# Splitting a weight-rounding step into a third that stays in place and two thirds that are issued later, in the first stage of an attention and mixture-of-experts kernel

## What is computed

```
xn = layernorm(x)
x  = x + attn0(xn) + ffn0(xn)      # attn0: 16 heads, latent projections, softmax, causal
                                   # ffn0: router, top 4 of 8 experts, gate/up, down
xn = layernorm(x)
x  = x + attn1(xn) + ffn1(xn)      # attn1: sparsemax; ffn1: grouped attention, then top 2 of 8 experts
```

## Time and profile before

| | |
|---|---|
| median of 3 runs | 3134.1 us (3131.94 to 3136.5) |
| the profiled execution | 3129.51 us, span of the core 3127.6 us |
| PE busy over the span | 2809.4 us (90%) |
| DVE, ACT, POOL busy | 2133.4 (68%), 1615.2 (52%), 1506.6 (48%) us |
| granted TensorE clock | 0.956 of full speed over the span, 0.79 in 60 to 350 us |
| in 60 to 350 us | PE busy 228.3 of 290 us, DVE 221.6, POOL 206.7, ACT 138.1 |

### The profile page before, as it was taken

The page is one execution under the profiler, slowest core; times in us unless marked ns, Lnnn a source line. Parts: engine busy times, 40 slices in busy tenths (PEclk is TensorE's granted clock), DMA queues, the critical chain, the costliest instruction groups (busy, mean ns, idle before and its releaser), DMA issues. The chain is left out here.

```text
span 3127.6 us, 61182 instructions
## 1 busy us (share of the span) xinstructions
PE 2809.4 (90%) x20990; PEld 2275.6 (73%) x20990; DVE 2133.4 (68%) x6013; ACT 1615.2 (52%) x3388; POOL 1506.6 (48%) x2213
## 2 busy tenths in 40 slices
PE   5877799999999999978998898998799999999996
PEld 3555478888899889846666666666588888888864
DVE  6878678788788788767777877766644444454565
ACT  3544344444454445545655555655455555555553
POOL 4768743443343354385556666322233333332487
PEclk8878799999999999989999999999899999999998
DMA  3555578788888888422333344210466666665355
GB/s 83 197 208 202 196 262 311 278 286 316 284 290 307 294 286 308 178 40 55 97 99 104 105 107 109 93 69 22 164 213 210 228 213 212 204 241 203 124 97 126
DMA packets 212008, 580.13 MB, mean 185 GB/s; under 512 B 24617, under 2 KB 146417, under 8 KB 167409
## 3 DMA queue, kind: packets, MB, share of 16 engines
q1 hardware_dynamic: 172528, 523.82, 47.7%
q0 software_dynamic: 36864, 51.14, 8.1%
q10 hardware_dynamic: 2304, 1.21, 0.1%
HBM read 450.14 MB, written 125.96 MB: 184 GB/s over the span
## 5 line engine op out<-in xcount | busy, mean ns | idle before, releaser
L1139 POOL TENSOR_TENSOR al<-t,ah 128x512 fp32r<-128x512 f32 x220 | 283.4, 1288 | 875.1 <-ACT ah L1375 875.1
L481 PE MATMUL bank<-xh,gu 128*128 128x256 f32 x3520 | 672.3, 291 | 33.6 <-DVE gc L1654 25.8
L481 PEld LDWEIGHTS bank<-xh,gu 128*128 128x128 f32 x3520 | 512.6, 190 | 57.7 <-issue 55.0
L524 PE MATMUL bank<-masks_bf,ident_bf 128*128 128x128 bf16 x1896 | 432.9, 252 | 133.9 <-DVE st L1840 41.0
L1840 DVE TENSOR_REDUCE st<-bank 128x1 f32<-128x512 f32 (+3 forms) x1024 | 422.1, 481 | 166.1 <-PE bank L542 158.6
L1472 ACT ACTIVATE pt<-bank 128x512 f32<-128x512 f32 (+1 forms) x1152 | 512.0, 540 | 30.2 <-PE bank L545 21.9
L524 PEld LDWEIGHTS bank<-masks_bf,ident_bf 128*128 128x128 bf16 x1896 | 170.3, 99 | 353.6 <-DVE st L1840 95.3
L1480 ACT ACTIVATE oT<-bank 128x512 f32<-128x512 f32 x192 | 114.6, 597 | 602.5 <-PE bank L621 576.5
L542 PE MATMUL bank<-ksT,qsT 128*128 128x512 f32 (+3 forms) x1536 | 410.3, 369 | 5.7 <-DVE top L1838 3.1
L545 PE MATMUL bank<-qaT,ksT 128*128 128x512 f32 (+3 forms) x1536 | 399.6, 372 | 0.0
L481 PE MATMUL bank<-xl,gu 128*128 128x256 f32 x1760 | 351.5, 281 | 0.0
(11 more groups left out here) (250 smaller groups left out, 5216.2 us busy)
## 6 DMA issues: line engine op xcount, KB each, us to landing
gu<-wu_scratch SPq DMA_DIRECT2D x110, 1032.0 KB, 5.2
gu<-wu_scratch SPq DMA_DIRECT2D x110, 1024.0 KB, 7.4
dn<-wd_scratch SPq DMA_DIRECT2D x110, 1024.0 KB, 6.7
xs<-xs_scratch SPq DMA_DIRECT2D x110, 264.0 KB, 4.3
ys_scratch<-yb SPq DMA_DIRECT2D x110, 256.0 KB, 7.0
raw<-in_gu SPq DMA_DIRECT2D x16, 1024.0 KB
wu_scratch<-hi SPq DMA_DIRECT2D x16, 1024.0 KB
wu_scratch<-lo SPq DMA_DIRECT2D x16, 1024.0 KB
```

What stands on the lines that cost most here:

```text
L481: mm = pe.matmul(bank[:, TS * h:TS * (h + 1)], gu[:, col:col + P], x[s % 2][:, TS * k:TS * (k + 1)], start=(n == 0), stop=(n == len(terms) ...
L524: return pe.matmul(S.bank((which, G, u))[:, diag:diag + P * len(unit)], ident_bf[:, :], masks_bf[:, side, 0:len(unit), :].rearrange("p n k ...
L1139: pool.tensor_tensor(em["al"][s % 2][:, m, :], em["t"][g % 2][:, :], em["ah"][s % 2][:, m, :].bitcast(F32), ALU.subtract).then_inc(al_read ...
```

## The change

`first_high` and `first_low` now handle one third q per call. The first third (q = 0) stays where all three were. On ScalarE the thirds 1 and 2 follow `probabilities`; on VectorE they follow `route_place`. SyncE's program, and what it waits for, is unchanged: the load of the next raw weights and the stores still wait for all three lo thirds.

```diff
-                def first_high(e):
-                    act.wait_ge(r_raw, 32 * (e + 1))
-                    if e >= 2:
-                        act.wait_ge(r_stored[e % 2], 64 * (e // 2))
-                    for q in range(3):
-                        sl = slice(third * q, third * (q + 1))
-                        act.activation(ro["hi"][e % 2][:, sl], ro["raw"][:, sl], ACT.Copy).then_inc(r_hi, 1)
+                def first_high(e, q):
+                    if q == 0:
+                        act.wait_ge(r_raw, 32 * (e + 1))
+                        if e >= 2:
+                            act.wait_ge(r_stored[e % 2], 64 * (e // 2))
+                    sl = slice(third * q, third * (q + 1))
+                    act.activation(ro["hi"][e % 2][:, sl], ro["raw"][:, sl], ACT.Copy).then_inc(r_hi, 1)
...
                     if routes(G, 1):
-                        first_high((G - 1) // 2)
+                        first_high((G - 1) // 2, 0)
...
                     probabilities(G, range(NU))
+                    if routes(G, 1):
+                        first_high((G - 1) // 2, 1)
+                        first_high((G - 1) // 2, 2)
...
-                def first_low(e):
-                    if e >= 2:
+                def first_low(e, q):
+                    if e >= 2 and q == 0:
                         dve.wait_ge(r_stored[e % 2], 64 * (e // 2))
-                    for q in range(3):
-                        sl = slice(third * q, third * (q + 1))
-                        dve.wait_ge(r_hi, 3 * e + q + 1)
-                        dve.tensor_tensor(ro["lo"][e % 2][:, sl], ro["raw"][:, sl], ro["hi"][e % 2][:, sl].bitcast(F32),
-                                          ALU.subtract).then_inc(r_lo, 1)
+                    sl = slice(third * q, third * (q + 1))
+                    dve.wait_ge(r_hi, 3 * e + q + 1)
+                    dve.tensor_tensor(ro["lo"][e % 2][:, sl], ro["raw"][:, sl], ro["hi"][e % 2][:, sl].bitcast(F32),
+                                      ALU.subtract).then_inc(r_lo, 1)
...
                     if routes(G, 2):
                         route_weigh((G - 2) // 2)
-                        first_low((G - 2) // 2)
+                        first_low((G - 2) // 2, 0)
...
                     if routes(G, 2):
                         route_place((G - 2) // 2)
+                        first_low((G - 2) // 2, 1)
+                        first_low((G - 2) // 2, 2)
```

## The result

The changed kernel takes 3161.82 us (median of 5 runs, 3154.6 to 3165.87), the kernel before beside it 3134.1 us (5 runs, 3127.1 to 3139.42): a ratio of 1.009, 95% interval 1.007 to 1.0109. It is 27.7 us slower where 14.7 were forecast, and 1.8 us above the upper end of the range. The interval of the ratio reaches from 22 to 34 us, so that the 1.8 us past the range say little, and the 13 us past the forecast are clear. The profiled execution has a span of 3159.9 us (3127.6 before).

The account below looks back on a forecast made before the run. No engine was taken as full; the loop lo, load, hi, oT, pt bounds, with the load issued later. Round delays of +11.7 us plus 3 for the clock gave 3134.1 + 14.7 = 3149 us, range 3132 to 3160.

Parts of the forecast that it names:

- the clock term: On TensorE, logits and bias matmuls slowed by low clock behind longer waits: 3 us taken from 0 to 14.5.
- Only rounds 0, 1 and 4 have much to lose: Reason for taking only 3 us for TensorE's clock: the other rounds were said to have little to lose.
- part of it meets POOL's slack: Second reason for only 3 us of clock loss: some falls where pairs wait for POOL anyway, 18.8 us of waits.
- The upper bound of 14.5 us: TensorE's clock loss if all logits and bias matmul sets fell to pair 13's times: 9.3 plus 5.2 us.
- the sum was about +26: Whole change if every TensorE burst after a wait starts at low clock: 11.7 us of delays plus 14.5.
- The mechanical sum: Delays over rounds 0 to 7 from the later load of raw, without the clock: +11.7 us.
- the list of what would show it: Trace signs: load about 5 us later, ScalarE's raw waits 30 to 45 us, heads_out waits under 5, pt waits 10 more.
- The credits: On ScalarE, two hi thirds behind pt let oT and pt start 1.9 us earlier after the load has landed.
- The third, the clock in full at 3160 us: Rival: TensorE's clock falls in every round, 14.5 us in place of 3, giving 3160 us; chance 0.08.
- The faster one: Rival: the load lands under 4.6 us after issue and heads_out's gain counts, 7.5 us in all, 3127 us; chance 0.12.
- The absorbed one: Rival: later waits take in half the delay of rounds 0, 3, 4 and 5, clock free, 3139 us; chance 0.20.

Follow-up runs that it names:

- The late load alone: Kernel before, no copy moved, with only the load of raw also waiting for the slots: 3133.59 us, ratio 1.0094 to the kernel before.
- The filler: Changed kernel plus 16 spare matmuls in each of pairs 3, 5, 9, 11 and 13, where TensorE waits for pt: 3140.78 us, 1.0035 of the kernel before.
- the two halves: Kernel before with only hi thirds 1 and 2 moved: 3103.19 us, ratio 0.9996; with only lo thirds 1 and 2 moved: 3134.0 us, ratio 1.0088.
- the lo half alone: Kernel before with only lo thirds 1 and 2 moved behind the slots, all hi thirds ahead of oT: 3134.0 us, ratio 1.0088.
- the controls: Four spare matmuls in each of the same five pairs: on the kernel before, 0.9991; on the changed kernel with raw loaded in thirds, 0.9967 (0.9965 without).

## Why the prediction was wrong

**The cause was right.** The price lies on SyncE: the load waits for the third lo, which had moved behind the slots. The late load alone gives the whole ratio (1.0094 against 1.009), and a load that waits only for its own third takes it away.

**The step that failed is the clock term: "I take 3 us, near the low end".** The filler, which leaves the load late, gives back 0.55% of the changed kernel's time, 17 us, with some 8 us either way by the two intervals; the trace by itself has 13.4 us more PE time for the same matmuls. Both are far above 3. Neither is the term itself: not all PE time need lie on the path, and the filler takes the two groups to 34.2 us, below the 43.2 of the trace of before, so part of its gain can be low clock that the kernel before has as well. So the term is put at 13 to 17 us only as an estimate.

The reason given had a right half and a wrong one. "Only rounds 0, 1 and 4 have much to lose" was right for the two groups counted: these three lost 9.2 of the 10.3 us. But then the term was 9 us by the rows and not 3, unless "part of it meets POOL's slack", and there was little of that: of PE's 18.8 us in the earlier trace rows 13.0 are the one at the start, which stays, and the other 5.8 are soon used up. The upper bound of 14.5 us held for the two kinds of matmuls that it was counted on, but they are not all: the scores and masks take 8.3 us more (q 4.0, k 1.9, masks 2.4), and the projections and the rest give back 5.2.

In each of rounds 0, 1, 3, 4 and 5 PE came to wait 3.6 to 5.4 us, with 3.42 and 3.78 us of matmuls behind it. The length of that one wait does not settle it: in round 6 of the changed kernel waits of 1.55 and 0.71 us have the same 3.42 and 3.78 behind them, and so has the 1.77 us of the earlier trace rows.

The Trainium skill ("TensorE: Matmul & The Clock Gate", section "HAM oscillation") has a matmul loop that waits between bursts start every burst at the low clock. By it the sum was about +26. This case's trace agrees, with 3.42 and 3.78 us behind each of the five waits; that the measured 27.7 us lies so near is in part luck, since the two groups gave 10.3 of its 14.5 us. I had set that rule at 0.08 on the ground that PE's shorter waits for heads_out keep the clock up. They did get shorter, 12.7 to 1.6 us, and it did not help.

**The mechanical sum came out right as a total, and not by its rounds.** With the filler the changed kernel is 0.35% slower, 11 us by 3130 (interval 7 to 15), against a sum of 11.7. The table has what each round added to the delay, from the start of its first lo third to that of the next (the last row: to the stores of blank rows), against the trace of before. The kernels before of the two groups differ by 4 us, so the last column is good to a few us.

| round | sum forecast, without the clock | changed kernel | with the filler |
|---|---|---|---|
| 0 | +3.3 | +10.9 | +7.8 |
| 1 and 2 | -0.6 | +0.9 | -5.9 |
| 3 | +3.2 | +4.7 | +1.2 |
| 4 | +3.3 | +5.5 | +2.7 |
| 5 | +3.3 | +3.2 | -0.3 |
| 6 | +0.3 | +3.3 | +1.6 |
| 7 | -1.1 | +4.1 | +4.2 |
| sum | +11.7 | +32.6 | +11.4 |

Round 0 cost more than twice its forecast even with the filler, though its oT was late by only 3.9 and 3.8 us (102.39 and 102.24 against 98.47), near the 3.3 forecast. The rest of that round's loss arises behind oT, which the prediction did not follow. Rounds 1 and 2 took in more than forecast, rounds 3 to 5 cost 3.6 us in all where 9.8 were forecast, and rounds 6 and 7 cost 5.8 where 0.8 were to be won. That the total fits to 0.3 us is luck. What the last two columns do show is that the two terms are not independent, and I had added them as if they were: where PE is fast, rounds 1 and 2 take in 5.9 us of the delay, and in the changed kernel nothing.

**By the list of what would show it.** SyncE issues the load 8.7 us behind the first lo third in rounds 0, 1, 4 and 5, where I had 8.5 (3.5 and 5.0 more); in round 3 it is 10.5, with VectorE's own 1.65 us wait ahead of heads_out. ScalarE's wait grew to 59.6 us in seven, not 30 to 45. PE's wait for heads_out fell under 5. Its wait for pt grew from 10.5 to 18.8 us; with those ahead of a fifth k unit that the view calls "issue" (1.06 and 1.77 us before, 5.04 after) it is 10.5 us more, and 10 or more were forecast. The load still lands after 7.4 to 7.8 us. All of the shift arises before 416 us (33 us, 32 at the end).

**The credits.** Three hi thirds to one was to give 1.9 us in each round; by the two halves it is worth nothing measurable. The mechanical sum has that credit in it four times, 7.6 us, so losses of like size must have been left out; those behind oT in round 0 and those of rounds 6 and 7 are the ones that the table shows.

**The rivals.** The third, the clock in full at 3160 us, came within 2 us, with the luck named above. The faster one is excluded by the landing. The absorbed one did not come even where PE was fast: with the filler 0.35% is left.

**What stays open.** Waits that the trace calls "remote" or "issue", such as VectorE's 1.65 us at 211.28 and PE's 5.04 at 228.69, have no releaser in the records; the second fits pt by its place only. Why the lo half alone costs no more than the whole change isn't settled. How the 27.7 us split into waits and clock is known only roughly: the filler gives back up to 17, and no run holds the clock of the changed kernel at just that of the kernel before.

## What to carry to other kernels

Before work that frees a buffer is moved behind other work, look at who waits for its last piece: here no engine's own order was hurt, only a load on a queue that the edit doesn't show. If the piece is split, split the wait and the transfer with it; that turned 1.009 into 0.9965. And where a change adds waits of 3.6 to 5.4 us on TensorE, as here, count the matmuls behind them at the time that rows at the low clock give, all kinds of them and in every round that isn't slow already, and don't count on idle time elsewhere to absorb the delay: slow matmuls spend it. Last, a sum that is right in total may be wrong in each round; the starts of the rounds are quickly compared.

## What was not expected of the hardware

Work that computes nothing made a kernel faster. Sixteen spare 128x512 matmuls in five pairs took the granted clock in 60 to 410 us to 0.81, in place of the changed kernel's 0.74 in 60 to 416, and the time down by 0.55%; where PE had no such wait, four of them did at most 0.2% (the controls). The two levels show directly in one group of instructions: 16 logits matmuls took 1.85 us in each round with the filler (14.8 in eight), and 3.42 us behind a wait of 5.04. With no edit at all, the kernel before took 3104 us at a mean granted clock of 0.962 in one group and 3130 at 0.957 in another (medians of 15 and 25 runs); whether the clock makes that difference no run shows.
